# Group 0's products moved in between the units that build the matrices, on one Trainium2 core

## The reference

```python
masked_w = weight * mask[None, :, :]                 # weight (8, 256, 256), mask (256, 256)
w_bot = jnp.einsum('bg,got->bot', y, masked_w)       # y is cond_8 (32, 8)
return x + jnp.einsum('bnt,bot->bno', x, w_bot) + bias   # x (32, 256, 256), bias (256)
```

## Time and profile before

| | |
|---|---|
| median of 3 runs | 68.54 us (68.35 to 68.59) |
| the profiled execution | 68.52 us, of which the span is 66.6 us |
| granted TensorE clock, mean | 0.998 |
| busy in the span | PE 60.5 us, DVE 47.4, ACT 47.6, POOL 7.8 |

### The profile page before, as it was taken

One profiled execution on the slowest core, in us unless ns is written; L12 is line 12 of the kernel. 1 busy time (PEld: TensorE's weight loads), 2 busy tenths in 40 slices (PEclk: granted clock), 3 DMA queues, 4 the chain that ended last, 5 costly groups with the idle time before them and its releaser, 6 DMA issues.

```text
span 66.6 us, 1494 instructions
## 1 busy us (share of the span) xinstructions
PE 60.5 (91%) x649; PEld 55.3 (83%) x649; DVE 47.4 (71%) x32; ACT 47.6 (71%) x38; POOL 7.8 (12%) x16
## 2 busy tenths in 40 slices
PE   2998999939899999999999999999999999999910
PEld 1326798729688899999999999999999999999900
DVE  2121899955939999999999999979999990250200
ACT  0700869744799999999999999999599946005520
POOL 5500765900070000000000000000000000000000
PEclk9999999999999999999999999999999999999999
DMA  0699999999994007987998999999998068717393
GB/s 0 202 400 407 409 412 421 418 418 418 423 409 197 15 0 182 428 330 281 246 261 239 421 453 396 413 438 411 413 411 350 17 278 352 285 39 315 145 372 113
DMA packets 5189, 20.20 MB, mean 303 GB/s; under 512 B 576, under 2 KB 1088, under 8 KB 4160
## 3 DMA queue, kind: packets, MB, share of 16 engines
q1 hardware_dynamic: 4752, 19.79, 76.8%
q10 hardware_dynamic: 432, 0.33, 1.6%
HBM read 11.73 MB, written 8.39 MB: 302 GB/s over the span
## 4 chain that ended last, share of the span: by engine, by line
PE 80%; DMA 7%; ACT 5%; issue 3%; SPq 1%
PE slots L347 20%; PE slots L348 20%; PE slots L346 20%; PE slots L369 11%; PE slots L280 8%; DMA weights<-in_weight 7%; ACT w_raw L412 5%; PE slots L274 2%; ACT weights L439 1%; SPq L174 1%
## 5 line engine op out<-in xcount | busy, mean ns | idle before, releaser
L346 PE MATMUL slots<-x_hi,w_hi 128*128 128x256 f32 x112 | 31.5, 281 | 0.0
L347 PE MATMUL slots<-x_lo,w_hi 128*128 128x256 f32 x112 | 31.3, 279 | 0.0
L348 PE MATMUL slots<-x_hi,w_lo 128*128 128x256 f32 x112 | 31.3, 279 | 0.0
L346 PEld LDWEIGHTS slots<-x_hi,w_hi 128*128 128x128 f32 x112 | 21.1, 188 | 0.0
L347 PEld LDWEIGHTS slots<-x_lo,w_hi 128*128 128x128 f32 x112 | 21.0, 188 | 0.0
L348 PEld LDWEIGHTS slots<-x_hi,w_lo 128*128 128x128 f32 x112 | 21.0, 188 | 0.0
L468 DVE TENSOR_TENSOR w_lo<-w_raw,w_hi 128x2048 fp32r<-128x2048 f32 (+1 forms) x8 | 16.1, 2018 | 1.2 <-ACT w_hi L397 1.2
L459 DVE TENSOR_TENSOR x_lo<-x_ring,x_hi 128x2048 fp32r<-128x2048 f32 (+1 forms) x8 | 16.1, 2018 | 0.6 <-ACT x_hi L391 0.6
L406 ACT ACTIVATE weights<-slots,smalls 128x1024 f32<-128x1024 f32 x11 | 11.9, 1109 | 5.7 <-PE slots L348 5.7
L391 ACT CAST x_hi<-x_ring 128x2048 fp32r<-128x2048 f32 (+1 forms) x8 | 13.5, 1691 | 0.9 <-DMA x_ring<-in_x 0.9
L397 ACT CAST w_hi<-w_raw 128x2048 fp32r<-128x2048 f32 (+1 forms) x8 | 13.5, 1689 | 0.3 <-DVE w_raw L486 0.3
(11 more groups left out here) (18 smaller groups left out, 9.4 us busy)
## 6 DMA issues: line engine op xcount, KB each, us to landing
x_ring<-in_x SPq DMA_DIRECT2D x8, 1024.0 KB, 10.3
out<-weights SPq DMA_DIRECT2D x15, 512.0 KB, 4.8
x_ring<-in_masked SPq DMA_DIRECT2D x4, 512.0 KB, 5.8
weights<-in_weight SPq DMA_DIRECT2D x4, 256.0 KB, 5.9
out<-weights SPq DMA_DIRECT2D x1, 256.0 KB, 2.4
masks_off<-in_mask_off ACTq DMA_DIRECT2D x1, 128.0 KB, 4.6
out<-weights SPq DMA_DIRECT2D x1, 128.0 KB, 2.4
out<-weights ACTq DMA_DIRECT2D x1, 128.0 KB, 2.1
```

Of the source, the lines that this page charges most:

```text
L346: nc.tensor.matmul(dst, wh, xh, start=(k == 0), stop=False)
L347: nc.tensor.matmul(dst, wh, xl, start=False, stop=False)
L348: last = nc.tensor.matmul(dst, wl, xh, start=False, stop=(k == KC - 1))
```

## The change

Group 0's products are cut in three parts. The first (h=0, batches 0 and 1, four matmuls) comes between units 5 and 6, the second (h=0, batches 2 and 3) after unit 7, the third is h=1. For this `w_raw` is laid out by batch, so that TensorE can read it directly and POOL's gathers go; the PSUM slots of units 6 and 7 and of the groups are renumbered so that the first part has a place (slot 1). ScalarE makes two high pieces of group 1's matrices (h=0) and takes out the early product between the copies of units 5 and 6; DVE makes the low pieces at the same place. The masks of units 0 and 1 travel in `smalls`, the rest of `masks_off` goes to SP's queue behind pair 1. The masking of each pair is cut in halves, and `x` of group 0 is loaded in halves, the first ahead of pair 3. Group 0's second half (h=1) is taken out by ScalarE instead of DVE.

```diff
-        w_raw = sb("w_raw", [P, RUNS, B, RT])
+        w_raw = sb("w_raw", [P, B, KC * O])
+EARLY = 6
         def product(g, h):
-            return slots[:, (2 * g + h) % SLOTS, :]
+            return slots[:, (2, 0, 3, 1)[(2 * g + h) % SLOTS], :]
+        def unit_slot(u, side):
+            if u < EARLY:
+                return slots[:, 2 * (u % 2) + side, :]
+            return slots[:, ((0, 2), (3, 1))[u % 2][side], :]
+        early = slots[:, 1, 0:BANK]
+        pieces = ((0, NB // 2, 0), (NB // 2, NB, 0), (0, NB, 1))
...
 SyncE
+            load_pair(0)
+            load_pair(1)
+            sp.dma_start(masks_off[:].rearrange("p u m r -> p (u m r)"), mask_off).then_inc(masks_off_loaded, 16)
+            load_pair(2)
+            load_half(0, NB // 2).then_inc(half_x_loaded, 16)
+            load_pair(3)
+            load_half(NB // 2, NB).then_inc(x_loaded[0], 16)
+            load_group(1)
-            sp.wait_ge(masked_by_pool, PAIRS - 1)
+            sp.wait_ge(masked_by_pool, 2 * (PAIRS - 1))
             load_group(XS - 1)
...
+                if g == 0:
+                    sp.wait_ge(first1_by_act, 1)
...
 GpSimd
+                for i in range(2):
+                    nc.gpsimd.tensor_tensor(blocks[:, 2 * j, half_of(i)], staged(j)[:, 0:BANK][:, half_of(i)],
+                                            staged(j)[:, BANK:SLOT][:, half_of(i)], ALU.mult).then_inc(masked_by_pool, 1)
-            gather(0, 1)
-            gather(0, 0)
-            gather(1, 0)
-            gather(1, 1)
...
 TensorE
+                elif u == EARLY:
+                    pe.wait_ge(raw_by_act, u)
+                elif u > EARLY:
+                    pe.wait_ge(raw_by_dve, u - 1)
                 identity(on)
                 identity(on + 1)
+                elif u > EARLY:
+                    pe.wait_ge(early_by_act, 1)
...
+            for u in range(EARLY):
+                weigh_unit(u)
+            pe.wait_ge(raw_by_act, EARLY - 1)
+            pe.wait_ge(raw_by_dve, UNITS // HO)
+            pe.wait_ge(half_x_loaded, 16)
+            multiply_first(early, 0, 0, NB // 2).then_inc(early_ready, 1)
+            for u in range(EARLY, UNITS):
+                weigh_unit(u)
+            pe.wait_ge(raw_by_act, UNITS - 1)
+            pe.wait_ge(x_loaded[0], 16)
+            multiply_first(product(0, 0)[:, BANK:SLOT], 0, NB // 2, NB).then_inc(products_ready, 1)
+            pe.wait_ge(raw_by_act, UNITS)
+            pe.wait_ge(raw_by_dve, UNITS)
+            multiply_first(product(0, 1), 1, 0, NB).then_inc(products_ready, 1)
...
 ScalarE
             for u in range(UNITS):
+                if u == EARLY:
+                    high_piece(0)
+                    high_piece(1)
+                    act.wait_ge(early_ready, 1)
+                    nc.scalar.activation(result(0, 0)[:, 0:BANK], early, ACT.Identity, bias=bias(0)).then_inc(early_by_act, 1)
...
             for lo in (0, NB // 2):
-                high_weights(1, lo, lo + NB // 2)
                 high_x(1, lo, lo + NB // 2)
+            high_piece(2)
             high_weights(2)
             high_x(2)
-            finish(0, 0, out0_by_act)
+            nc.scalar.activation(result(0, 0)[:, BANK:SLOT], product(0, 0)[:, BANK:SLOT], ACT.Identity,
+                                 bias=bias(0)).then_inc(out0_by_act, 1)
             high_x(3)
+            finish(0, 1, first1_by_act)
             high_weights(3)
...
 VectorE
+                if u == EARLY:
+                    low_piece(0)
+                    low_piece(1)
...
             for lo in (0, NB // 2):
-                low_weights(1, lo, lo + NB // 2)
                 low_x(1, lo, lo + NB // 2)
+            low_piece(2)
             low_weights(2)
             low_x(2)
-            finish(0)
```

More of the change, by code:

```diff
@@ L138, in raw_slot, with raw_part, part @@
             half = u * SPAN // P
[L139 to L146, removed]
+            at = (half if diagonal else 1 - half) * O + u * SPAN
+            return w_raw[:, :, at:at + SPAN].rearrange("p b (m r) -> p m b r", r=RT)
+        pieces = ((0, NB // 2, 0), (NB // 2, NB, 0), (0, NB, 1))
+        def raw_part(g, lo=0, hi=NB, h=None):
+            v = w_raw[:, NB * g + lo:NB * g + hi, :]
+            return v if h is None else v.rearrange("p b (k o) -> p b k o", k=KC)[:, :, :, h * P:(h + 1) * P]
+        def part(w, g, lo=0, hi=NB, h=None):
+            v = w[:, g % (RS if w is w_hi else LS), lo:hi]
+            return v if h is None else v.rearrange("p b (k o) -> p b k o", k=KC)[:, :, :, h * P:(h + 1) * P]
         def part_x(v, lo, hi):
             return v.rearrange("p (k f) -> p k f", k=KC)[:, :, lo * N:hi * N]
-        def w_first(h, k):
-            return weights[:, h + 1, :].rearrange("p (b k o) -> p b k o", b=NB, k=KC)[:, :, k, :]
         def result(g, h):
@@ L321, in multiply_group @@
                 pe.wait_ge(x_lo_ready, 1 if g == 1 else g + 1)
-                pe.wait_ge(w_lo_ready, 1 if g == 1 else g + 1)
+                pe.wait_ge(w_lo_ready, 1 if g == 1 else g + len(pieces) - 1)
                 for h in range(HO):
@@ L338, in multiply_group @@
                             pe.wait_ge(w_lo_ready, 2)
+                        if g == 1 and h == 1 and b == 0:
+                            pe.wait_ge(w_lo_ready, len(pieces))
                         if g == GROUPS - 1 and h == 1 and b == NB - 1:
@@ L391, in high_x, with high_weights, high_piece @@
                 nc.scalar.copy(part_x(x_hi[:, g % RS], lo, hi), part_x(x_ring[:, g % XS], lo, hi)).then_inc(x_hi_ready, 1)
-            def high_weights(g, lo=0, hi=NB):
+            def high_weights(g):
                 if g > RS:
                     act.wait_ge(products_ready, HO * (g - RS + 1))
-                nc.scalar.copy(part(w_hi, g, lo, hi), raw_part(g, lo, hi)).then_inc(w_hi_ready, 1)
+                nc.scalar.copy(part(w_hi, g), raw_part(g)).then_inc(w_hi_ready, 1)
+            def high_piece(i):
+                nc.scalar.copy(part(w_hi, 1, *pieces[i]), raw_part(1, *pieces[i])).then_inc(w_hi_ready, 1)
             def finish(g, h, done):
@@ L453, in _ @@
             dve.wait_ge(masked_loaded[0], 16)
-            nc.vector.tensor_tensor(blocks[:, 0, :], staged(0)[:, 0:BANK], staged(0)[:, BANK:SLOT], ALU.mult).then_inc(masked_by_dve, 1)
+            for i in range(2):
+                nc.vector.tensor_tensor(blocks[:, 0, half_of(i)], staged(0)[:, 0:BANK][:, half_of(i)],
+                                        staged(0)[:, BANK:SLOT][:, half_of(i)], ALU.mult).then_inc(masked_by_dve, 1)
             def low_x(g, lo=0, hi=NB):
@@ L460, in low_x, with low_weights, low_piece @@
                                         part_x(x_hi[:, g % RS], lo, hi).bitcast(F32), ALU.subtract).then_inc(x_lo_ready, 1)
-            def low_weights(g, lo=0, hi=NB):
-                dve.wait_ge(w_hi_ready, 1 if (g == 1 and lo == 0) else g + 1)
+            def low_weights(g):
+                dve.wait_ge(w_hi_ready, g + len(pieces) - 1)
                 if g > LS:
                     dve.wait_ge(products_ready, HO * (g - LS + 1))
-                nc.vector.tensor_tensor(part(w_lo, g, lo, hi), raw_part(g, lo, hi), part(w_hi, g, lo, hi).bitcast(F32),
+                nc.vector.tensor_tensor(part(w_lo, g), raw_part(g), part(w_hi, g).bitcast(F32),
+                                        ALU.subtract).then_inc(w_lo_ready, 1)
+            def low_piece(i):
+                dve.wait_ge(w_hi_ready, i + 1)
+                nc.vector.tensor_tensor(part(w_lo, 1, *pieces[i]), raw_part(1, *pieces[i]), part(w_hi, 1, *pieces[i]).bitcast(F32),
                                         ALU.subtract).then_inc(w_lo_ready, 1)
@@ L532 @@
     t_off = mask.reshape(UNITS, SPAN, KC, P)
-    mask_off = np.concatenate([t_off[u, :, 1 - u * SPAN // P].T for u in range(UNITS)], axis=1)
+    first_off, mask_off = (np.concatenate([t_off[u, :, 1 - u * SPAN // P].T for u in units], axis=1)
+                           for units in (range(SIDES), range(SIDES, UNITS)))
     y = np.zeros((TILES, RT, G, B, RT), np.float32)
```

113 lines of the change are left out of this document (56 added, 57 removed).

## The result

The changed kernel took 67.88 us in the median of 12 runs (67.50 to 68.31), the kernel before 68.36 us in 12 (68.07 to 68.81). The ratio is 0.9919 with a 95% interval of 0.9892 to 0.9945, so it is faster by 0.8%, about 0.5 us. Ratios here are not the quotients of the medians and differ a little from them. Up to three of ten executions of a run fell in a slower state of the chip, and medians, ranges and ratios leave these out. Forecast were 67.25 us and 1.3 us. The profiled execution is one of the slower ones: 68.21 us with a span of 66.3.

The account below looks back on a forecast made before the run. TensorE was taken to bound the kernel, with a 1.12 us hole in unit 6. Start 0.2, hole 1.12, small waits about 0.3, less 0.3 at group 4 gave 1.3 us off, so 67.25 us; range 66.8 to 68.2.

Parts of the forecast that it names:

- The hole: TensorE, unit 6: 1.12 us of "issue" read as a late program block, to be filled by the early products.
- The early products, units 6 and 7, group 0: TensorE: early products from 12.83 us, unit 6 at 14.70, group 0 ends and group 1 starts at 22.64 (24.26 before).
- ACT's list: ACT from its first piece to `high_x(4)`: 13.65 us instead of 14.01, so `high_x(4)` starts only 0.20 us earlier, at 32.06.
- 17 ACT instructions: The argument against full gain: the wait at group 4 rests on this many ACT instructions whose durations barely vary.
- DVE's relief from `finish(0)`: DVE loses `finish(0)`, which was said not to help, since DVE waits for ACT's `high_x(4)` anyway.
- Does it last?: ACT and DVE behind TensorE: group 4 due at 39.44 must wait until 39.75; the end comes 1.3 us earlier.
- the wait at group 4: TensorE waits at group 4 for DVE's low part of the matrices: a hole of 0.3 us near 39.5.
- the 0.06 of the prediction: Group 4: DVE's `low_weights(4)` ends at 39.69 and TensorE starts at 39.75.
- The start: Units 0 to 5: 96 KB less ahead of `weight[0]` in the queues gains 0.2 us, bounds 0 and 0.3.
- the 1.3 us of the sum: Whole span: 0.2 start, 1.12 hole, about 0.3 small waits at units 6 and 7, less 0.3 wait at group 4.
- the rivals: Four cases beside the forecast: 66.85 us (chance 0.12), 67.5 to 68.1 (0.16), 68.35 (0.11), slower at 68.9 or 70.7 (0.07).
- part of it: Rival: the block comes at 15.0 to 15.4, or units 6 and 7 wait for pieces; 67.5 to 68.1 us, chance 0.16.

Follow-up runs that it names:

- the third: Third profile of the changed kernel, no edit, on the same chip as the other third-sample runs: 67.66 us (4 runs), ratio 0.9877.
- the second profile: The changed kernel once more, no edit: 67.80 us (10 runs), ratio 0.9918; unit 0 fast in this profile.
- the small warm-up: Kernel before with its 9 warm-up matmuls of 512 columns as 36 of 128: 67.55 us (4 runs), 67.76 us (10 runs).

## Why the prediction was right in direction and too large

- *The hole* was a late block of the program, and the early products hide it: right. It follows the instruction count (two runs), comes back at its old place without the early products and their numbering (one), and escapes them when it is moved ahead (one). In the changed kernel 221 matmuls and 221 loads are done by 15.48, when unit 6 starts, so the place is at the end of the early products, as forecast.
- *The early products, units 6 and 7, group 0* were right to 0.15 us in the profile of the changed kernel with a fast unit 0, with group 1 at 22.68 for 22.64. ACT's and DVE's pieces fit. I had missed that the slot numbers bring a wait of 1.16 us of their own; it costs nothing where the early products stand.
- *ACT's list* was right to the hundredth: 13.65 us from its start to `high_x(4)` in two profiles, 13.63 in the third. The prediction speaks of 17 ACT instructions; in the earlier trace rows 17 is DVE's count and ACT has 23, which changes nothing in the sum. That DVE's relief from `finish(0)` doesn't help was right too.
- *Does it last?* This is the step that failed in size. I put the wait at group 4 at 0.31 us; it is 0.60, 0.63 and 0.61. In the second profile ACT's list started 0.1 us later than forecast, so the low part was done 0.1 later (39.79), TensorE's next start was due 0.1 earlier (39.33 for 39.44), and taking the stream up again costs 0.17 instead of the 0.06 of the prediction, for which no row stands. The due time was mis-read: 24.26 is where the chain of the earlier trace rows puts group 1, but in the timeline the starts lie ahead of that. Group 4 of the kernel before started at 40.91 and not at 41.06, as its timeline shows:

```profile
40.91 0.28 PE L346 MATMUL slots<-x_hi,w_hi 128*128 128x256 f32 x1
```

  Three terms of 0.1 on one side double the wait. The whole wait is the price of the one part of the change that moves `finish(0, 1)` to ACT: without it the kernel gains about 0.5 us more (67.88 and 67.80 to 67.35 and 67.32).
- *The start* is the other step that failed, and in sign. I took 0.2 us for the earlier weights and nothing for TensorE's clock in unit 0, which the prediction doesn't mention. In the profile with a fast unit 0 the 0.2 us are there. But in three profiles of the changed kernel unit 1 began at 7.11, 6.44 and 6.94 us, against 6.62 and 6.63 before: in two of them TensorE was still at 1.2 GHz when the weights came. On average of the three that is 0.2 us lost instead of gained. Whether the change makes the slow unit 0 more frequent isn't shown. Both profiles of the kernel before had a fast one, but with the small warm-up it too had one of 1.36 us (the first of its two profiles), and the first profile of the changed kernel (68.21 us) is among its slower executions.
- The two terms are 0.3 and 0.4 us. With them the 1.3 us of the sum become 0.6, and 0.5 were measured. What is left is within the scatter, and includes the late pair 3 and the spacing below; how often each occurs I can't say from one profile in each run.
- Of the rivals, none took place by its mechanism. The range held, but its likeliest part, 67.0 to 67.5, did not: 67.88 lies where I had put the rival "part of it", which was to come from a later block or from waits in units 6 and 7. Neither is seen: from the start of the early products to the second stretch of L398 are 4.33 and 4.32 us in the first two profiles, for 4.45 in the forecast. That the range held is luck.

## What to carry to other kernels

A hole in TensorE with no wait behind it can be a block of its program that comes late. Move it by changing the number of instructions ahead of it and see whether it follows; that costs one run, and here it gained as much as the rewrite. When work is moved off the chain, recount the list of the engine that follows at a distance (here ACT, whose `high_x(4)` came 0.1 us earlier than before in the fast profile, where TensorE was 1.6 us earlier): one instruction of 1.01 us added to that list cost half of the gain. A forecast that ends in the difference of two long sums, due time and done time, needs the cost of stopping and restarting added (0.17 us here) and a range as wide as the sums' errors.

## What the runs showed of the hardware

- A block of TensorE's program comes late by up to 1.13 us. TensorE stops each time behind the same 222 loads and goes on 2.3 to 2.6 us behind the start of the instruction packet. The Trainium skill (Runtime: NRT & Kernel Launch, Instruction fetch mechanics) says that crossing such a boundary is mostly hidden. It holds for the later packets of every profile here and not for the first. That the full DMA engines are the reason isn't shown: at 18 to 19 us they were as full, 96.8% of their time on data in the kernel before, and the packet there made no hole. What also differs is the pace. Between the first packet and the hole TensorE went through 54 loads and matmuls in 1.5 us; at 18 to 19 us it worked on 13 in 1 us. No run separates the two.
- TensorE's step from 1.2 to 2.4 GHz came at very different moments. In the changed kernel it came ahead of unit 0 in the second profile, and in the first, as the lengths of unit 0's records show (416 ns up to 6.68 us, 269 from 6.89), at about 6.8 us. With 11 warm-up matmuls all were over sooner than 9 in the profile after; their starts are 0.427 us apart up to the seventh and 0.216 from the eighth, which puts the step at about 4.0 us. The column of the granted clock says 1.00 throughout.

```profile
1.19 3.94 PE L392 MATMUL slots<-zeros 128*128 128x512 bf16 x11 [1.19 <-DVE zeros L509]
```

```profile
1.19 4.02 PE L392 MATMUL slots<-zeros 128*128 128x512 bf16 x9 [1.19 <-DVE zeros L509]
```

- The spacing of the matmuls in groups 1 to 7 is 0.1167 us in most profiles. From group 4 on it is 0.1178 in one of the changed kernel, 0.9% more, behind the wait. From the first start of group 4 to the last matmul one needs 62.88 - 40.51 = 22.37 us, the other 62.46 - 39.89 = 22.57, with equal work:

```profile
62.88 0.28 PE L385 MATMUL slots<-x_hi,w_lo 128*128 128x256 f32 x1
```

```profile
62.46 0.28 PE L385 MATMUL slots<-x_hi,w_lo 128*128 128x256 f32 x1
```

  In two other profiles it is 0.1178 from group 1 on, which is 0.4 us over all groups. The cause is open.
